# Window attention and a gated depthwise mix on one core: ScalarE's second exponentials placed ahead of the attention output rows in the joined strips

## The reference, cut to what matters

```python
# layer 0
x = layernorm2d(x0, ln_w, ln_b)                      # over channels
q, k = split(conv1x1(x, qk_w, qk_b)); vs = conv1x1(x, vs_w, vs_b)
local = depthwise3x3(vs) + depth_b
v1, v2 = vs[:, :48], vs[:, 48:]
q, k, v1 = roll(q, -4), roll(k, -4), roll(v1, -4)     # shifted 8x8 windows, 4 heads
y = roll(softmax(q @ k.T * SCALE) @ v1, 4)
y = concatenate([y, v2])
s = (y + local).mean(axis=(2, 3))                    # over a whole image
ca = sigmoid(fu2 @ leaky_relu(fu1 @ s, 0.2))
y = conv1x1(y * ca + local * (1 - ca), proj_w, proj_b) + x0
# layer 1: a 3x3 depthwise filter whose 4 live taps come from the image's mean of y
out = depthwise3x3(y, filters(mean(y))) + bias
```

## Time and profile before

| what | value |
|---|---|
| median of 3 runs | 1529.0 us (1526.08 to 1533.34) |
| the profiled execution's own time | 1525.35 us |
| its span in the profile | 1523.8 us |
| TensorE busy (matmuls) | 1404.1 us, 92% |
| VectorE busy | 1315.9 us, 86% |
| ScalarE busy | 875.5 us, 57% |
| GpSimd busy | 251.0 us, 16% |
| DMA engines, mean share | 52.9% |

### The profile page before, as it was taken

The page is one execution under the profiler, slowest core; times in us unless marked ns, Lnnn a source line. Parts: engine busy times, 40 slices in busy tenths (PEclk is TensorE's granted clock), DMA queues, the critical chain, the costliest instruction groups (busy, mean ns, idle before and its releaser), DMA issues.

```text
span 1523.8 us, 34270 instructions
## 1 busy us (share of the span) xinstructions
PE 1404.1 (92%) x10355; PEld 878.2 (58%) x10355; DVE 1315.9 (86%) x2350; ACT 875.5 (57%) x2279; POOL 251.0 (16%) x741
## 2 busy tenths in 40 slices
PE   5999999989999999999999999999999999978886
PEld 3667677666656666556556666656666656522332
DVE  3566565569999999999999999999999999999998
ACT  2565655566666666666656666676666676522221
POOL 2111111112221222202111221112212112100000
PEclk9999999999999999999999999999999999999999
DMA  2121221165556655665566555665556555678885
GB/s 61 50 80 54 58 75 54 57 144 140 135 141 161 153 144 140 144 151 144 134 143 161 149 144 131 155 154 133 135 153 158 144 135 142 161 173 209 202 198 129
DMA packets 81354, 203.02 MB, mean 133 GB/s; under 512 B 15248, under 2 KB 19112, under 8 KB 81320
## 3 DMA queue, kind: packets, MB, share of 16 engines
q1 hardware_dynamic: 81320, 202.60, 52.9%
HBM read 136.57 MB, written 64.91 MB: 132 GB/s over the span
## 4 chain that ended last, share of the span: by engine, by line
PE 47%; DVE 32%; issue 12%; DMA 5%; ACT 3%; DVEq 1%; ACTq 0%; SPq 0%; POOL 0%; POOLq 0%
DVE mixed L1182 12%; PE banks_t L557 8%; PE banks_s L521 6%; DMA qd<-nmx 5%; PE banks_g L496 5%; PE banks_t L529 4%; DVE bn L979 4%; PE banks_a L557 4%; PE banks_g L618 4%; PE banks_g L504 3%; PE banks_g L611 3%; DVE oo L1193 3%; DVE mx L1008 3%; PE banks_g L613 3%; DVE xn L1000 3%
## 5 line engine op out<-in xcount | busy, mean ns | idle before, releaser
L1182 DVE SCALAR_TENSOR_TENSOR mixed<-vin,c_pack,mixed 96x1024 f32<-96x1024 f32 x352 | 451.7, 1283 | 6.5
L1193 DVE SCALAR_TENSOR_TENSOR oo<-zs,l_w,oo 96x1024 f32<-96x1024 f32 x192 | 245.6, 1279 | 9.8 <-ACT oo L846 4.1
L810 ACT ACTIVATE pt<-banks_t 128x512 f32<-128x512 f32 x256 | 138.6, 593 | 109.7 <-PE banks_t L529 108.2
L1008 DVE TENSOR_REDUCE mx<-banks_s 128x8 f32<-128x512 f32 x260 | 167.0, 684 | 21.8 <-PE banks_s L521 17.6
L521 PE MATMUL banks_s<-km,qd 64*128 64x128 f32 x2080 | 152.9, 286 | 23.3 <-issue 13.8
L521 PEld LDWEIGHTS banks_s<-km,qd 64*128 64x128 f32 x2080 | 129.6, 189 | 77.7 <-DVE mx L1008 48.7
L788 ACT ACTIVATE vd<-banks_a 64x192 f32<-64x192 f32 x260 | 87.1, 335 | 138.7 <-PE banks_a L510 133.9
L434 POOL COPY vrow<-vw 96x16 f32<-96x16 f32 (+2 forms) x520 | 165.3, 373 | 0.0
L529 PE MATMUL banks_t<-qd,km 64*128 64x128 f32 x2048 | 150.3, 287 | 15.0 <-DMA qd<-nmx 14.5
L611 PE MATMUL banks_g<-vin,proj_t 128*96 128x512 f32 (+1 forms) x288 | 147.2, 611 | 12.5 <-DMA ycat<-y_img 7.0
L979 DVE BATCH_NORM_STATS2 bn<-banks_a 128x6 f32<-128x96 f32 x528 | 98.8, 247 | 62.4 <-PE banks_a L471 62.1
(11 more groups left out here) (148 smaller groups left out, 1999.6 us busy)
## 6 DMA issues: line engine op xcount, KB each, us to landing
vin<-v_img SPq DMA_DIRECT2D x64, 495.0 KB, 6.0
v_img<-vrow SPq DMA_DIRECT2D x130, 198.0 KB, 2.7
xc<-in_x SPq DMA_DIRECT2D x134, 192.0 KB, 2.6
x<-in_x SPq DMA_DIRECT2D x64, 384.0 KB, 7.1
out<-oo SPq DMA_DIRECT2D x64, 384.0 KB, 3.0
y_img<-ybuf SPq DMA_DIRECT2D x128, 99.0 KB, 2.0
ycat<-v_img SPq DMA_DIRECT2D x64, 198.0 KB, 4.9
ycat<-y_img SPq DMA_DIRECT2D x64, 198.0 KB, 6.9
```

The lines of the kernel that those rows point to most:

```text
L1008: v.tensor_reduce(mx[:, n, :, 4 * r:4 * r + 4].rearrange("q h e -> q e h"), banks_s[:, n, :].rearrange("q (e h k) -> q e h k", h=2, k=K), ...
L1182: v.scalar_tensor_tensor(out=mb[:C, par, :, 0:W], in0=vin[:C, par, 1 + dh:1 + dh + WS, 1 + dw:1 + dw + W], scalar=depth_w[:, DVE_TAPS[m]:D ...
L1193: v.scalar_tensor_tensor(out=oo[:, par, :, :], in0=zs[:, at:at + WS, 1 + dw:1 + dw + W], scalar=l1_w[:, n:n + 1], in1=oo[:, par, :, :], op ...
```

## The change

In the joined strips ScalarE's `exps(t, 1)` moves from behind `y_out(t - 1)` to ahead of it. Nothing is added or removed. The other engines' lists and ScalarE's `alone` stay as they are. Strips without attention have no `exps` and stay as they are as well.

```diff
@@ -909,10 +909,11 @@
                     exps(t, 0)
                     vs_out(t + 1, 0)
                     vs_out(t + 1, 1)
+                if attend:
+                    exps(t, 1)
                 if y:
                     y_out(t - 1, 1 - k, h - 1 + k)
                 if attend:
-                    exps(t, 1)
                     if gated is not None:
                         sigmoid_exp(gated)
                     keys(t + 1, 1 - k)
```

## The result

The changed kernel takes 1614.1 us (median of 4 runs, 1608.2 to 1618.2), the kernel before beside it 1530.1 us. The ratio is 1.0544, with a 95% interval of 1.0517 to 1.0570: 84 us slower. The forecast was 1599 us, between 1556 and 1618. The profiled execution takes 1612.23 us, 86.9 more than that of before.

A forecast was written before the change was run, and what follows sets the result against it. TensorE, nearly full in joined strips, and the chain from `y_out` through SyncE's loads to the move of the maxima were the bounds; 17 + 38 + 10 + 5 = 70 us gave 1599 us as median, range 1556 to 1618.

The forecast's parts named there:

- Rival (c): Joined strips' 0.30 us gap ahead of the scores is a hidden wait that goes: 1515 us; chance 0.05 with no effect.
- TensorE's path: Joined strips: later queries delay the score matmuls and second scores, costing 0.62 us per strip, 30 us over 48 strips.
- SyncE can't catch up: SyncE's list behind the y store: all eleven DMA issues move by 1.79 us, with no other wait to absorb it.
- The move lands with the loads: Move of the maxima follows the end of the loads, landing 1.79 us later; room 0 to 0.6 us per strip.
- Rival (a): Move doesn't wait for loads; only TensorE's 30 us counts: 1559 us; chance 0.17 with values up to the forecast.
- one queue in order: SyncE's DMA rings: descriptors consumed in order put the move behind the loads, 4.61 us against 1.97 us free.
- First loop: 14 joined strips of the first loop: 1.79 us less 0.5 room, 1.2 us each, 17 us.
- Later loop: 28 joined strips: 21 already waiting for the move lose 1.79 us each, 38 us; other 7 lose 10 us.
- The other six strips: Strips 16, 17 and the first two of two later images: 0.9 us each, 5 us.
- ScalarE's first tap: The mixing's first tap on ScalarE waits for vin's load, 1.8 us later, but is hidden by idle time: no cost.
- The granted clock stays: TensorE would be busy some 20.5 of 23 us, 89%, so its granted clock was expected not to change.
- rival (b): Every joined strip pays 1.79 us or more, 86 us and up: 1615 us and more; chance 0.06.

The follow-up runs named there:

- e11: Changed kernel with the y store issued behind loads and move of the maxima, and that move ahead of x0's load: 1550.6 us, ratio 1.0151.
- e10: Kernel before with the y store issued behind loads and move of the maxima, and that move ahead of x0's load: 1517.3 us, ratio 0.9926.
- e5: Half dose against the kernel before: second exponentials placed after the first two of five output-row copies in joined strips; 1572.6 us, ratio 1.0318.
- e1: Changed kernel, but in joined strips SyncE issues the y store behind the loads and the move of the maxima: 1556.5 us, ratio 1.0169.
- e2: Kernel before with only the loads late: SyncE's y store waits for the next strip's first half of keys; 1635.4 us, ratio 1.0717.
- e4: Changed kernel, but ScalarE issues the move of the maxima in a queue of its own in joined strips: 1609.2 us, ratio 1.0530.
- e7: Changed kernel, but SyncE issues the move of the maxima ahead of x0's load: 1561.2 us, ratio 1.0221.
- e8: Kernel before, but SyncE issues the move of the maxima ahead of x0's load: 1517.6 us, ratio 0.9945.
- e3: Changed kernel plus one useless 0.86 us matmul per joined strip where TensorE waits for the move of the maxima: 1600.5 us, ratio 1.0460.
- e9: Kernel before with only the loads late, plus a useless matmul where TensorE waits for the move of the maxima: 1595.2 us, ratio 1.0415.

## Why the prediction was right, point by point

- **ScalarE's new idle time**, 0.79 us forecast: 0.68 us. **`y_out`'s end**, 7.4 us after the start: 7.36.
- **Nothing gains** from the earlier exponentials: e11 against e10 shows only loss. Rival (c) had no wait to remove.
- **TensorE's path**, 0.62 us per strip, 30 us: 0.54 to 0.6 us per strip and 33 us in all (e11 against e10). The 33 us hold some 27 us at full clock; the rest comes with the lower clock (e10 and e11). The wait ahead of `values` was 0.50 instead of 0.6 us, and the scores stand 0.10 us behind the queries, as forecast.
- **SyncE can't catch up**: x0's load 15.88 instead of 14.13 us after the start, +1.75 against 1.79. e5's 1.04 gives a loss as well.
- **The move lands with the loads**: shown by e1, e2 and e5. Rival (a) is refuted. The mechanism that I gave for it, one queue in order, is refuted by e4; e7 and e8 fit that what was issued ahead must be worked off, also from another queue. The Trainium skill ("DMA: Bandwidth & Descriptors", "Queues, rings and completion order") states order within one ring; that rule alone would have let the move of e4 pass, and it took 5.4 us. The same section says that the semaphore's increment lands only after every earlier write of the same DMA engine, across its queues. e4's 5.4 us agree with that, but no run here tells it from another cause that holds the move.
- **First loop**, 1.2 us per strip: 22.4 / 14 = 1.6, and 1.35 without the long strip (292.3 / 13 = 22.49 against 21.14). The room of 0.5 us that I read was about right.
- **Later loop**, 48 us for 28 strips, 1.7 each: 26.8 + 28.3 = 55.1 us for 27 strips, 2.0 each. Of these 1.2 + 3.1 + 2.7 + 1.5 = 8.5 us lie in four strips at the lower clock; without that excess it is 1.7 each. One count in this term was wrong: of the 21 waits of before only 17 stand ahead of these 28 strips, two ahead of strips 16 and 17 and two ahead of strips 48 and 49. With 17 and 11 strips the same prices give 45 us instead of 48.
- **The other six strips**, 5 us: strips 16 and 17 alone cost 5.0 us, at a lower mean clock, and 32, 33, 48 and 49 together 1.8.
- **ScalarE's first tap, nothing**: its waits for vin's load grew from 11.2 to 42.2 us in all. In e7 they are still 38.5 us, and e7's strips without a wait for the move or a fall of the clock take 21.45 and 21.80 us, as in e11 without them. They are hidden, as forecast.
- **"The granted clock stays"** is the step that failed. I had reasoned from a mean busy share of 89%. The clock fell after single waits for the move, mostly of 1.6 to 2.2 us, and the mean over the execution went from 0.99 to 0.976. Two falls of after, and those of e7 and e11, came in the middle of strips. This is worth about 14 us or more (e3) and by the estimate there at most 23 us, which is the size of the gap between 70 us forecast and 87 us measured. It is also why rival (b), with its 1615 us, is nearer to the 1614 us measured than the forecast of 1599: its 1.79 us per strip are met on average (77.5 us in the 41 strips of the three stretches, 1.9 each), but only with the lower clock, which it doesn't name; without the 12 us of the five long strips it is 1.6.

The shares by the runs: some 27 us TensorE's own path at full clock, about 14 us or more the lower clock, and the rest of the 84 us the waits for the move beyond that path. They don't add up strictly, since a shorter path makes the waits longer, as e2 shows.

## What to carry to other kernels

When an instruction is moved in one engine's list, look up what waits for everything that it is moved past, and follow that into the DMA queue: here ScalarE's output rows head a list of eleven DMA issues, and 1.8 us there cost twice what TensorE's own path did. Try a small transfer on the critical path ahead of the last large load instead of behind it: here that paid in both kernels, and a queue of its own didn't. Where new waits come up on a TensorE that was full, count with its clock too: most falls in these runs followed waits of 1.6 us and more, and some came in strips whose only new wait was 0.5 us.

## What the runs showed of the hardware that was not expected

- A transfer of 16 KB takes 1.97 us with little beside it, and where TensorE waits for it behind 1.7 MB of loads 4.3 to 7 us, on SyncE's queue and on ScalarE's alike (5.4 us in e4). With 384 KB of these issued behind it instead of ahead it is in time in e8, and in most strips of e7. What holds the move in the second queue wasn't found.
- TensorE's granted clock falls to 0.50, for 3.4 or 6.8 us, after some waits of 1.6 to 2.9 us in an otherwise full stretch (after and e2), and not after others of the same length: in after 1.85 and 2.20 us had a fall behind them, 1.87 and 1.72 us had none. It also fell in the middle of strips in which TensorE was busy 22.2 of 23.0 us (e11) and had waited no longer than 0.50 us. One matmul of 0.86 us in the wait, of no use otherwise, was worth 14 us (e3) and 40 us (e9).
